# A graph network and linear attention kernel: keys and edge scores moved from the first pass into the edge loop

## The reference, cut to what matters

```python
xn = layernorm(x)
z = xn @ W_func.T;  h_s = xn @ W_self.T
e = leaky_relu(concat([z[src], z[dst], attr]) @ W_att.T)      # one score for each edge
alpha = segment_softmax(e, dst)
gnn = xn + relu(where(deg > 0, h_s + segment_sum(alpha * z[src], dst), xn))
q, k, v = xn @ Wq + bq, xn @ Wk + bk, xn @ Wv + bv            # 8 heads of 32
kv = sum over nodes of phi(k) (outer) v;  k_sum = sum over nodes of phi(k)
mix = layernorm(xn + attention(phi(q), kv, k_sum) @ Wo + bo)
mix = layernorm(mix + relu(mix @ W1 + b1) @ W2 + b2)          # 256 -> 1024 -> 256
x1 = x + gnn + mix (as the kernel adds them);  out = x1 + experts(layernorm(x1)), two of six experts a row
```

## Time and profile before

| what | us |
|---|---|
| median of 3 runs (2153.22 to 2165.94) | 2163.18 |
| profiled execution: span, first to last instruction | 2147.1 |
| profiled execution: time of its own | not given on the page |
| first gather of rows | 232.10 |
| first step's matmul | 309.64 |
| last gather of rows | 1549.83 |

### The profile page before, as it was taken

The page is one execution under the profiler, slowest core; times in us unless marked ns, Lnnn a source line. Parts: engine busy times, 40 slices in busy tenths (PEclk is TensorE's granted clock), DMA queues, the critical chain, the costliest instruction groups (busy, mean ns, idle before and its releaser), DMA issues.

```text
span 2147.1 us, 36524 instructions
## 1 busy us (share of the span) xinstructions
PE 1831.1 (85%) x9283; PEld 1382.1 (64%) x9283; DVE 1476.4 (69%) x3838; ACT 1069.7 (50%) x3294; POOL 1339.2 (62%) x1102
## 2 busy tenths in 40 slices
PE   6899637888888998999899988889987789999991
PEld 5555425666666666666666666666654469989981
DVE  6989426767777776777677777777766657445574
ACT  2444334556555555555555555555544345555550
POOL 5000577887888888888888888888700444764276
PEclk9999858989998888888888899888888889999996
DMA  8999355555555565656566555555519644655464
GB/s 197 294 275 300 89 140 130 148 150 150 151 149 153 149 159 147 158 155 164 148 164 160 153 150 150 151 151 151 134 55 243 177 123 134 169 162 153 135 182 122
DMA packets 312784, 344.98 MB, mean 161 GB/s; under 512 B 127407, under 2 KB 270490, under 8 KB 309455
## 3 DMA queue, kind: packets, MB, share of 16 engines
q1 hardware_dynamic: 169765, 198.42, 33.4%
q0 software_dynamic: 135840, 137.77, 25.9%
q10 hardware_dynamic: 6975, 6.45, 1.0%
HBM read 254.64 MB, written 86.69 MB: 159 GB/s over the span
## 4 chain that ended last, share of the span: by engine, by line
PE 58%; DVE 14%; issue 9%; POOL 8%; DMA 7%; DVEq 2%; ACT 1%; SPq 1%; POOLq 0%; ACTq 0%
PE bank L710 55%; POOL wexp L663 6%; DMA wexp<-func_rows,a_src 4%; DVE acc L1881 4%; DVEq L1881 1%; DVE wexp L1464 1%; POOL g_all L697 1%; DMA g_all<-sorted_d 1%; PE bank L1047 1%; DVE work L1638 1%; SPq L406 1%; PE bank L858 1%; DVE acc L1467 1%; POOL acc L675 1%; DMA work<-mix_rows 0%
## 5 line engine op out<-in xcount | busy, mean ns | idle before, releaser
L663 POOL DMA_INDIRECT wexp<-func_rows,a_src x850 | 1046.3, 1231 | 437.8 <-issue 196.5
L710 PE MATMUL bank<-wexp,onehot 125*125 125x257 f32 x1700 | 601.4, 457 | 93.2 <-DVE acc L1881 82.4
L1881 DVE SCALAR_TENSOR_TENSOR acc<-acc,corr,bank 125x257 f32 x850 | 400.1, 471 | 266.8 <-PE bank L710 234.5
L1201 ACT ACTIVATE onehot<-iota_r,a_rel 125x125 f32<-125x125 f32 x850 | 335.1, 394 | 430.4 <-PE bank L710 427.8
L710 PEld LDWEIGHTS bank<-wexp,onehot 125*125 125x125 f32 x1700 | 322.8, 215 | 236.8 <-ACT onehot L1209 133.4
L1209 ACT ACTIVATE onehot<-onehot,a_p 125x125 f32<-125x125 f32 x850 | 327.9, 386 | 0.8 <-DVE a_p L1840 0.8
L687 POOL DMA_INDIRECT sorted_d<-acc,work x100 | 122.1, 1221 | 221.8 <-DVE acc L2016 140.0
L710 PE MATMUL bank<-g_all,wexp 128*128 128x128 f32 x1840 | 226.6, 276 | 3.1 <-ACT g_all L1342 2.1
L710 PEld LDWEIGHTS bank<-g_all,wexp 128*128 128x128 f32 x1840 | 216.1, 193 | 4.9 <-ACT g_all L1342 2.4
L710 PE MATMUL bank<-work,w_s 128*128 128x250 f32 x800 | 206.6, 380 | 4.1 <-ACT work L1192 2.6
L697 POOL DMA_INDIRECT g_all<-y_d,work x100 | 131.0, 1310 | 114.4 <-DVE g_all L2186 62.2
(11 more groups left out here) (271 smaller groups left out, 2565.8 us busy)
## 6 DMA issues: line engine op xcount, KB each, us to landing
rel_oh<-rel_d SPq DMA_DIRECT2D x50, 531.2 KB, 6.0
wexp<-in_attr SPq DMA_DIRECT2D x25, 896.0 KB
sorted_d<-spare SPq DMA_DIRECT2D x72, 256.0 KB, 6.4
g_all<-sorted_d SPq DMA_DIRECT2D x115, 128.0 KB
y_d<-g_all SPq DMA_DIRECT2D x115, 128.0 KB, 2.9
wexp<-func_rows,a_src POOLq DMA_INDIRECT x850
work<-xn_rows SPq DMA_DIRECT2D x38, 224.0 KB
xnT_d<-work SPq DMA_DIRECT2D x25, 250.0 KB, 9.0
```

What stands on the lines that cost most here:

```text
L663: pool.indirect_dma_start(ring[:, n % RING, :], None, func_rows, bass.IndirectOffsetOnAxis(ap=a_src[:, n // CS, n % CS:n % CS + 1], axis=0 ...
L710: return pe.matmul(o, l, r, start=first, stop=last_, **kw)
L1201: act.activation(onehot[:, n % AHEAD, :], iota_r[:], ACT.Abs, bias=a_rel_v[:, n:n + 1], scale=-1.0).then_inc(s("far"), 1)
L1881: v.scalar_tensor_tensor(to, to, corr[:, k % 2, y:y + 1], bank[3 + n % 2][0:R, 0:D + 1], ALU.mult, ALU.add).then_inc(s("summed"), 1)
```

## The change

The first pass makes only func rows, the transposed rows, and each row's mean and scale, which now stay in SBUF. What it no longer does:

- Keys are made in the edge loop from `xnT_d`, at the steps in `KV` (groups 0 to 5 at steps -36 to -31, then one every 4 or 5 steps up to step 51). Only phi(k) times the normalised row is summed, and phi(k) itself; the values' weights are applied once at the end (`kv_whole`, at step 53).
- Normalised rows are no longer stored in the first pass. ACT makes them again from `x` where they are used (`kv_parts`, `m_affine_x`, `m_whole`), and `xn_out` stores them from the loop.
- Edge attributes are multiplied and summed in 100 pieces of 8 lists (a quarter of a former chunk): eight ahead of the loop, the rest one every 8 steps from -36 to 692. The scores go to DRAM in list order; each run loads a window of 66 lists and a product with a 0/1 matrix (`sel`, `ew_w`) picks its rows inside `turn_scores`. The ten indirect transfers go.
- The mix of group g starts at step 56 + 30 g (`MIX0`, `PERIOD`) and takes 62 steps; DVE's two multiplications and additions by row are fused with centring and scaling.
- Tables of steps are made from one-hot matrices with 16 matmuls instead of 80; table work is spread over the groups.
- The last group's mix ends inside the loop (step 838).

```diff
-BY_DVE = dict(oh0=0, oh1=1, oh2=2, oh3=3, u0=8, ...
+BY_DVE = dict(oh0=0, oh1=1, oh2=2, oh3=3, sel=6, u0=8, ...
+PIECE_AT = [None] * FIRST + [8 * p - 100 for p in range(FIRST, ALL_PIECES)]
+KB, PB, KK = 4, 3, (0, 1, 5)
+KV = [-LEAD + g for g in range(6)] + [-28 + g * 84 // 19 for g in range(GROUPS - 6)]
+KV_END = KV[-1] + 2
+MIX0, PERIOD = 56, 30
...
 (SP, ahead of the loop)
+            for g in range(3):
+                kv_in(g)
+            sp.wait_ge(s("gates"), 4)
+            load("tables_out", by_run(gate_d), gates[:, TABLES + 2:, :])
+            attr_in(2)
...
+            relative_in(0)
+            attr_in(3)
+            kv_in(3)
+            attr_in(4)
+            ew_out(0)
+            attr_in(5)
+            run_in(0)
+            attr_in(6)
+            attr_in(7)
+            attr_in(8)
+            ew_out(1)
+            attr_in(9)
+            for k in range(LOADS_MIX):
+                mix_weights(k)
...
 (POOL)
-            for n in range(RUN):
-                step_rows(n)
-            pool.wait_ge(s("ew_out"), 16)
-            for c in range(CS):
-                pool.indirect_dma_start(ew_l[:, c * R:(c + 1) * R], None, ew_d,
-                                        bass.IndirectOffsetOnAxis(ap=tab_i[:, 0, c:c + 1], axis=0)
-                                        ).then_inc(s("ew_in"), 16)
-            for n in range(RUN, STEPS):
+            for n in range(STEPS):
                 step_rows(n)
...
 (PE)
+            def keys_part(g, j):
+                if j == 0:
+                    pe.wait_ge(s(f"kv_in{g % KB}"), 48 * (g // KB + 1))
+                freed(pe, s("phi"), 2 * g + j - len(KK) + 1)
+                to = bank[KK[(2 * g + j) % len(KK)]][0:R, 0:D]
+                for c in range(2):
+                    mm(to, k_xT[g % KB][:, c, j * R:(j + 1) * R], wk_s[:, c, :], c == 0, False, skip_group_check=True)
+                mm(to, ones_p[0:PART, 0:R], bk_q[:], False, True, skip_group_check=True).then_inc(s("kv_ps"), 1)
+            def kv_sum(g):
+                pe.wait_ge(s("xn_made"), 2 * (g + 1))
+                for j in range(2):
+                    pe.wait_ge(s("phi"), 2 * g + j + 1)
+                    for c in range(2):
+                        mm(bank[7][:, c * D:(c + 1) * D], k_x[g % KB][:, j, c * 128:(c + 1) * 128], p_phi[g % PB][:, j, :], ...)
+                    last = mm(bank[6][0:1, 0:D], ones_c[0:R, :], p_phi[g % PB][:, j, :], ...)
...
-                pe.transpose(k_turn, k_u[:], ident[0:R, 0:R]).then_inc(s("k_pe"), 1)
+                mm(k_turn, k_u[:], ident[0:R, 0:R], True, False)
+                mm(k_turn, sel[0:rows_, h, :], ew_w[0:rows_, h, :], False, True).then_inc(s("k_pe"), 1)
...
+            for n in range(-LEAD, STEPS):
+                for g in kv_at(n):
+                    keys_part(g, 0)
+                    keys_part(g, 1)
+                    if g:
+                        kv_sum(g - 1)
+                if n == KV_END:
+                    kv_sum(GROUPS - 1)
+                    kv_whole()
+                for g, at in mix_at(n):
+                    if at == 1:
...
+                        queries(g)
+                    if at == 10:
+                        attention(g)
+                    if at == 12:
+                        self_part(g)
+                    if at == 18:
+                        project(g)
+                    if at == 27:
+                        turn(g)
+                    if 0 <= at - PERIOD - 3 < FC:
+                        hidden(g, at - PERIOD - 3)
+                    for z, j, h in ((13, 0, 0), (15, 0, 1), (18, 1, 0), (20, 1, 1)):
+                        if at == PERIOD + z:
+                            down(g, j, h)
...
 (DVE; ahead of the loop edge_piece(0) to edge_piece(7))
+            def edge_piece(p):
+                h, c, q = p % 2, p // PIECES, p % PIECES
+                v.wait_ge(s(f"attr_in{h}"), 32 * (p // 2 + 1))
+                v.tensor_tensor(attr_s[:, h], attr_s[:, h], awe[:, None, :].to_broadcast([R, EDGES, ED]), ALU.mult)...
+                v.tensor_reduce(ew_c[:, c % 2, q * EDGES:(q + 1) * EDGES], attr_s[:, h], AX.X, ALU.add)...
+            def m_centred(own, z, mv_, k):
+                for j in range(2):
+                    own.did(v.scalar_tensor_tensor(z[:, j], z[:, j], mv_[:, j, 0:1], rv[:, k, :], ALU.subtract, ALU.mult))
+                for j in range(2):
+                    v.scalar_tensor_tensor(m_y[:, j], m_z[:, j], rstd[:, j:j + 1], rv[:, 2, :], ALU.mult, ALU.add)...
+            (positions in the group: clip 3, sum 5, biased 8, den 11, inverse 12 and 13, quotient 14, residual 19,
+             spread 20 and 21, mean and variance 22, centred 23, normed 25, keep 27; second half: down 53, spread 54 and 55,
+             mean and variance 56, centred 58, normed 60, last 62)
```

1066 lines of the change are left out of this document (500 added, 566 removed).

## The result

| | kernel before | changed kernel |
|---|---|---|
| median | 2158.20 us of 4 runs (2151.69 to 2165.94) | 2195.72 us of 4 runs (2193.60 to 2203.72) |
| ratio of the changed kernel | | 1.018, 95% interval 1.0159 to 1.0201 |
| profiled execution, span | 2147.1 | 2191.9 (its own time 2193.60) |

What follows compares the result with a forecast made beforehand. PE and DMA were taken to bind the first pass, POOL the edge loop, with PE/DVE nearly as slow. Last step 1578 instead of 1606.7, less 3.5 of leftover, gave -32 us: span 2115, time 2131 us, range 2045 to 2195.

Steps and rivals of the forecast that it cites:

- the carry to the time: The old kernel's median lay 16.1 us above its profiled span; this was added unchanged to the forecast span.
- 1, first gather: First pass: groups 3.0 us apart, first gather at 97 us instead of 232, bounds 85 and 112.
- 2, first step: From first gather to first step: 62 us for 13 key groups plus 33 us of waits, 95 us; bounds 63 and 135.
- rival C: Stage from first gather to first step takes its upper bound, 135 us; time 2171 us; chance 0.10.
- only the first step is late: The sign by which rival C was to be recognised: the first step alone comes later than forecast.
- 3, steps 0 to 56: Start of the edge loop: twelve more key groups, steps, scores and key-value product take 110 us, to 302 us.
- 4, periods: Loop periods of 30 steps: 49.6 us each, 49.1 after the pieces end; 24 take 1188 us, the first 40.
- 5, the end: Last 44 steps take 48 us, last step at 1578; DVE's 3.5 us leftover goes, later stages stay the same.
- 6, ScalarE, SP and DMA hidden: In the loop, ScalarE's row copies, SP's requests and 38 MB more DMA traffic cost nothing; uncovered copies up to 43 us.
- The port rule: DVE work sharing ports with GpSimd could hold POOL's gathers, at worst 114 us; the forecast took nothing for it.
- A (POOL stays the pace): Loop periods stay at POOL's 46.1 us, 82 us less in all; 2049 us; chance 0.23.
- B: DVE's additions to each period's light part show in full, period 52.0 us; 2189 us, deciding from 50.8; chance 0.23.

Runs made afterwards that it cites:

- spread: Changed kernel with the products of each key group from group 13 on dealt out over four steps, one part a step; 2151.22 us, ratio 0.9992.
- sums: Changed kernel with the sum of phi over the rows moved from PE to DVE additions, one product with ones at the end; 2172.72 us, ratio 1.0098.
- w_late: Changed kernel with the 20 weight loads moved in SP's queue from ahead of the loop to one a step in steps 0 to 19; 2159.67 us, ratio 1.0029.
- lead: Changed kernel with weight loads in steps 0 to 19, edge pieces 4 to 8 among the first key groups, fifth and sixth groups' rows requested earlier; 2151.72 us, ratio 0.9989.
- no_pieces: all4 without the multiplication and sum of edge pieces from piece 10 on, so edge scores are not the reference's; 2061.22 us.
- gathers10: Changed kernel with ten more indirect gathers on POOL, their rows thrown away, behind the first 17; 2185.99 us, ratio 1.0149.
- all4: Changed kernel with the edits of lead, sums and spread together; 2111.13 us, ratio 0.9814.

## Why the prediction was wrong, step by step

**What bounds the kernel now, and the carry to the time.** The reading of the kernel before stands. Carrying 16.1 us from the span to the time did not: in the changed kernel's run the two are 1.7 us apart, and the 16 were the scatter between runs. The stages are therefore 77 us off where the time is 65 off.

**1, first gather.** Right in size: 101.85 for 97 us, within 85 to 112. ACT and its issues set the pace, as chosen, at 2.53 us a group; stops for DVE's tables (5.36 us at 47) make it 3.4 on average.

**2, first step.** This is the step that failed first, 129 us for 95, inside its bounds (135). Two terms were mis-sized. The group: 4.8 us were ten products at 0.43, read from a row of four products (eight matmuls) whose drains overlap; two by two between short bias and sum products a product took 0.53, and a group 5.8, with scores 6.2. For 13 groups that is 18 us. The waits: 33 us were counted for weight loads and pieces together, where they came to 20.5 + 16.7 plus 4.5 at the start; the loads held SP for 30 us, not 13. The last 8 us or so are, by subtraction, products at the low clock behind those waits. By rival C's place and price (135 us, 2171) this was C, and "only the first step is late" did not hold, for the next stage was late too. Behind the 16.68 us wait two products took 2.07 us, and 1.13 later; with this the trace agrees with the rule named there (the Trainium skill, TensorE: Matmul & The Clock Gate, HAM oscillation), that a PE which waits for data starts again at the low clock.

**3, steps 0 to 56.** This is the step that failed most for what it is, 142 us for 110, and together with step 2 it makes up 67 of the 77 us. The work was counted and the order was not. I let 12 steps run "right behind such products at 0.43" and 44 "at 0.85", as if it made no difference which products stand beside a step and what DVE's additions and the clock do between them. spread shows that it does: with the same instructions dealt out, the stage takes 111.4 us, and the kernel loses its disadvantage, 0.9992. The clock is below its upper level there with short waits alone: sums shows no wait of PE over 3.0 us, a mean clock of 0.84, and two products at 2.07 us and at 1.13 within 12 us. The Trainium skill (TensorE: Matmul & The Clock Gate, A second HAM failure mode: psum-queue depth-cycling) describes such a case, a kernel that cycles through PSUM banks with brief idle times between its groups of matmuls and whose clock swings between its levels. The trace agrees that it swings; what decides how often is open, since w_late had 0.87 and lead 0.94 with the same products and the same waits.

**4, periods.** Right in size, 48.67 for 49.6, dense part 33.9 for 34.6, light part 14.9 for 15.0, but in part by luck: two errors cancel. The pieces cost 1.8 us a period (48.86 to 47.08), 1.3 in the light part and 0.4 in the dense one, where the sum had 0.5 for them, and without them the period was 47.1 where the sum had 49.1. DVE's extra mix work in the light part seems hidden (13.6 without pieces; the lower end was 13.7), but no run took it out by itself. The pieces show by 40% of their DVE time, almost wholly in the light part, of which a third had been taken. The first period was taken at 40 us, which is the length without pieces (39.0 in no_pieces); with them it is 45 to 46.

**5, the end.** Last 44 steps right, DVE's leftover gone. The 555.4 us behind were scatter.

**6, ScalarE, SP and DMA hidden.** True in the 24 periods for SP and DMA: PE's wait table has DVE's additions, 73.7 us in 118 times, and next ScalarE, 25.8 us in 34 times, none over 1.8 us. In the loop of the kernel before ScalarE had 8.9 us. So its price was small but not nothing, 1.1 us a period now. In the lead it was SP's queue. The port rule that spoke against DVE work beside gathers shows nowhere: 1.54 us a gather beside the pieces of the lead, 1.52 in the quiet stretch before. Its worst case of 114 us was also too high by half, since by the rule as told there only the multiplication of a piece has two inputs, and the sum over the piece doesn't.

**The rivals.** A (POOL stays the pace) fell: POOL waited 225.6 us, and ten transfers more cost nothing (gathers10). B's mechanism is real and its place is right (DVE is 95% busy in the light part shown, and pieces show there almost wholly), but the period stayed under 50.8, from where it decides. C was the nearest, at 0.10 given too little. What none of the cases had: a loss in steps 0 to 56.

Why then the whole is slower. The last step of the kernel before came at 1606.3 us, and POOL set it: its 34-step periods took 52.24 us on average over twenty, which is 34 gathers at 1.536. The change starts POOL 130 us earlier, but moves 25 x 5.8 = 145 us of PE's work for keys behind that start, in front of a loop where PE has little to spare. Take away the lead's two waits, deal the products out, give the key sums to DVE, and the same design ends its last step at 1563.8 us; with 28 steps a period it is 2.6% faster than the kernel before.

## What to carry to other kernels

When a change frees the engine that sets the pace, first ask which engine is second and what the change adds to it: here POOL got 130 us of head start, and PE got 145 us of work behind that start, about half of it ahead of its first step. Work that is put into a loop of short, mutually waiting steps is best dealt out one piece a step, so that each hand-over has something beside it: the order alone was worth 27 to 30 us in a stage of 138 to 141. And loads that nobody needs yet don't belong ahead of those that somebody waits for in one queue; count the queue's issue time too (30 us for 20 loads), not only the bytes. Once the engine behind them is faster, look again: in all4 PE waited 6.3 us for rows among the same loads, moved later.

## What the runs showed of the hardware that I had not expected

- With the same products in steps 0 to 56 and the same waits (13.1 to 13.9 us, none over 2.2), the mean granted clock was 0.93 to 0.95 in five profiles and 0.87 in w_late, and PE was busy 119.4 to 122.6 and 129.7 us.
- In sums PE lost about 12 us of products in that stage, and the stage took 145.4 us: waits for DVE of 20.2 us, the longest 3.0, and a mean clock of 0.84. One profile, so a sign only.
- In that stage of sums the same two products took 1.13 us at the upper level of the clock (2.4 GHz) and 2.07 at the lower one (1.2 GHz), 12 us apart.
- Twenty loads of 3.7 MB held SP's queue for 30 us, one load of a single row (bv_r) for 8.88 us of it, at a DMA share of 0.93 over the loads.
- Two key products (four f32 matmuls) took 1.06 us to the next operation between two bias products and 0.96 behind a step's product, at the same upper level of the clock.
- A stretch of about 548 us behind the loop, with the same 2948 matmuls, came out between 540.8 and 555.4 us in fourteen profiles.
